# Four graph layers on one core: products copied by ScalarE, parts summed by TensorE, roots by Newton steps on VectorE, and one more tick between steps

## The chip, the cores and the metric

The kernel runs on one core of a Trainium2 chip. The metric is the device time of one launch in microseconds (us), taken as the median of several runs. PE is TensorE, PEld its weight loads, DVE VectorE, ACT ScalarE, POOL GpSimd and SP SyncE.

## The reference

Four graph networks run one after the other on 50,000 nodes of 256 numbers, each as `x = layernorm(x + net(x))`; all share one list of 25,000 edges. The first is a hypergraph net, the second and the fourth are two graph attention (GAT) convolutions each, the third is a graph convolution with batch norm. One GAT convolution:

```python
h = (x @ W).reshape(n, HEADS, HID)
e = leaky_relu(a_s[src] + a_d[dst], 0.2)
m = segment_max(e, dst); ex = exp(e - m[dst])
alpha = ex / segment_sum(ex, dst)[dst]
out = segment_sum(h[src] * alpha[:, :, None], dst) + b
```

The second net puts `elu` behind both of its convolutions. In the fourth the first convolution ends in a layernorm and a relu, and the second has one head.

## The kernel before

Nodes are kept in 98 tiles of 512 rows (128 partitions x J = 4 rows x 256 numbers, fp32). Region 0 (49 tiles) holds the nodes that edges point to, in the order of the edges; region 1 (49 tiles) the nodes that no edge points to, so they need no neighbours. `ORDER` mixes the two regions, mostly by turns. Edges are worked in 25 batches of up to 8 columns, two tiles of region 0 each.

After two hypergraph phases and two phases of node work, the program has five calls of `layer_phase`, each a `Block` of its own in which all engines start together: **l1** (kind `l1a`: second net, softmax sum and elu of its first convolution, and the product with the weights of its second), **l2** (`l1b`: sum and elu of the second, residual, layernorm), **l3** (`gcn`), **l5** (`l3a`: fourth net, sum, layernorm, relu, product) and **l6** (`l3b`: last sum, residual, layernorm, rows scattered to the output). Between l3 and l5 runs a phase of node work alone.

In a layer phase each engine runs its own program over a common count of ticks. The table `L` of class `Nodes` gives each stage of a tile its tick: tile u is at stage s in tick u + L[s]. No engine waits at a tick's end; it waits only on semaphores of other engines' steps. If a result is asked for in the same tick in which it is made, the asking engine usually waits; one tick later it usually does not. On DVE the steps of a tick are generators, and `take_turns` issues one instruction of each by turns, so that a step in a chain of dependent ones lies beside others.

Stages of a tile: `load` (SP); `pre` (ACT scales half of the tile's own rows by their share, L2283, DVE the other half, L2356, and DVE weighs the neighbours' sum into `part`, L2352, and adds it, L2371); ACT's exp for elu (L2261); `body` (elu L2395, in l2 also the residual L2405; row statistics L2421); `var` and `norm` (the variance, its root as `pow` on POOL L2135, DVE's `shifts` L2443, then ACT's normalized rows `z` L2248); `turn` and `zt` (PE transposes, ACT copies them, L2231); `prod` (PE, L2170, two halves of PSUM, `pm`); `evict` (out of PSUM: DVE with a bias row `row_b` in l1, L2454 and L2456; ACT in l5); `store` (SP, in l6 POOL's scatters, L2142).

Edges, batch b at tick `at(b)`: POOL gathers rows (L1667, each a software DMA for 128 rows), DVE makes the logits and running maxima at `at - 3` (L1824 to L1844), ACT their exps (L1733), DVE weighs and accumulates (L1865, L1881), ACT copies the maxima beside the sums at `at + 1` (L1737), SP stores them at `at + 2`, DVE makes the shares.

## Time and profile before

| | |
|---|---|
| median of 3 runs | 7084.83 us (7073.76 to 7100.17) |
| the profiled execution, its own time | 7096.27 us |
| its span, first to last instruction | 7094.5 us |
| DVE busy | 4901.1 us, 69% of the span |
| POOL busy | 3995.6 us, 56% |
| PE busy | 3822.3 us, 54% |
| ACT busy | 3205.9 us, 45% |
| mean granted PE clock | 0.799 |

Busy shares over the whole span hide that the phases have different limits; they are read phase by phase below. In the windows each row is a stretch of the span with each engine's busy us and its count of instructions, the granted PE clock (0.50 is 1.2 GHz, 1.00 is 2.4 GHz), the mean share of the DMA engines, and GB/s. One fp32 matmul of the program shows as two MATMUL rows, a transpose as one.

### The profile page before, as it was taken

To read this page: it belongs to the slowest core of one execution; us is meant where nothing else is said; L and a number is where in the kernel's file an instruction comes from. 1 tells how busy PE (TensorE), PEld (TensorE's weight loads), DVE (VectorE), ACT (ScalarE), POOL (GpSimd) and SP (SyncE) were. 2 spreads that over 40 slices of the span, in tenths; PEclk is the share of its full clock that TensorE was granted. 3 is DMA by queue.
4 is the path that set the end of the run, shared out by engine and by line. 5 is a ranking of instruction groups with operands and counts; after the bars stand their busy time and mean duration, and the time that the engine had idled before them with its cause. 6 is when DMAs were issued, how large, how long until landed. Compare 5 with 4: busy or idle time off the path is not lost. (4 is left out here: it accounts for less than half of the span.)

```text
span 7094.5 us, 77303 instructions
## 1 busy us (share of the span) xinstructions
PE 3822.3 (54%) x18205; PEld 3003.3 (42%) x18205; DVE 4901.1 (69%) x15616; ACT 3205.9 (45%) x7082; POOL 3995.6 (56%) x3216
## 2 busy tenths in 40 slices
PE   3568881068885887477700005998885677600000
PEld 1257770057774666366600002546774566500000
DVE  6635454634456776799799996866665999576664
ACT  0023330023333554355445555768885788633333
POOL 4767776757774887544065525621112555278887
PEclk9789995589997998799955557999998899855555
DMA  8744446945446997777578878989996677576665
GB/s 306 283 93 77 76 69 206 382 86 78 75 69 209 350 349 284 210 257 263 185 261 291 290 260 287 382 296 330 332 336 221 232 250 240 178 254 224 231 223 191
DMA packets 646102, 1633.93 MB, mean 230 GB/s; under 512 B 128454, under 2 KB 283878, under 8 KB 630290
## 3 DMA queue, kind: packets, MB, share of 16 engines
q1 hardware_dynamic: 459954, 1234.83, 49.9%
q0 software_dynamic: 185696, 394.18, 20.7%
q8 instruction: 150, 2.46, 0.2%
q14 instruction: 302, 2.47, 0.1%
HBM read 816.50 MB, written 813.62 MB: 230 GB/s over the span
## 5 line engine op out<-in xcount | busy, mean ns | idle before, releaser
L1708 PE MATMUL l_pb<-l_jx,k_ones 128*128 128x128 f32 x26 | 7.0, 446 | 1520.8 <-DVE l_jx L1941 1520.8
L802 POOL DMA_INDIRECT NS<-e_tot,e_idx x392 | 648.4, 1654 | 292.2 <-ACT e_tot L1060 221.2
L2248 ACT ACTIVATE l_z<-l_a,l_nb,l_rs 128x256 f32<-128x256 f32 x1176 | 609.8, 598 | 394.3 <-DMA out_dram<-l_z,k_ids 382.0
L1667 POOL DMA_INDIRECT l_eg<-HBT,k_nsrc x392 | 497.8, 1270 | 366.4 <-POOLq L142 129.8
L1708 PEld LDWEIGHTS l_pb<-l_jx,k_ones 128*128 128x128 f32 x26 | 5.8, 326 | 1521.5 <-DVE l_jx L1941 1521.5
L936 DVE TENSOR_SCALAR e_eq<-e_pk,z_skey 128x128 f32<-128x128 f32 x588 | 203.8, 347 | 632.2 <-DMA NS<-e_tot,e_idx 606.6
L2135 POOL TENSOR_TENSOR l_rs<-l_ve,k_minus_half 128x8 f32<-128x8 f32 x147 | 279.5, 1901 | 447.6 <-ACT l_z L2248 327.1
L2142 POOL DMA_INDIRECT out_dram<-l_z,k_ids x392 | 420.5, 1073 | 119.4 <-issue 109.7
L2170 PE MATMUL l_pm<-k_w_L3b,l_zt 128*128 128x258 f32 x1568 | 404.4, 416 | 130.3 <-ACT l_o L2218 115.2
L1203 POOL DMA_INDIRECT XH<-n_o,z_home x392 | 401.3, 1024 | 120.2 <-issue 113.5
L1060 ACT ACTIVATE e_tot<-e_pa 128x520 f32<-128x520 f32 x196 | 118.5, 604 | 755.5 <-DMA NS<-e_tot,e_idx 743.2
L2421 DVE BATCH_NORM_STATS2 l_bs<-l_a 128x6 f32<-128x256 f32 x1176 | 447.1, 406 | 1.7
L2170 PE MATMUL l_pm<-k_w_L1b,l_zt 128*128 128x264 f32 x1568 | 403.6, 406 | 79.6 <-DVE l_o L2456 76.7
L2283 ACT ACTIVATE l_a<-l_a,l_eshare 128x64 f32<-128x64 f32 (+1 forms) x1372 | 379.6, 365 | 100.1 <-DVE l_eshare L1923 72.5
L1881 DVE SCALAR_TENSOR_TENSOR l_erun<-l_erun,k_same,l_eg 128x260 f32<-128x260 f32 (+2 forms) x880 | 417.8, 475 | 4.0
L1227 PE MATMUL n_pm<-z_w_L1a,n_zt 128*128 128x264 f32 x1568 | 397.9, 410 | 15.1 <-DVE n_o L1265 9.5
L1667 POOL DMA_INDIRECT l_eg<-XH,k_psrc x196 | 236.6, 1207 | 299.8 <-DVEq L1886 239.7
L2170 PEld LDWEIGHTS l_pm<-k_w_L3b,l_zt 128*128 128x128 f32 x1568 | 321.0, 210 | 191.7 <-issue 141.1
L1011 PE MATMUL e_po<-z_w_e2n,e_hid 128*128 128x256 f32 x1584 | 381.1, 384 | 24.5 <-DVEq L899 24.5
L1420 POOL TENSOR_TENSOR n_rs<-n_ve,k_minus_half 128x8 f32<-128x8 f32 x49 | 80.2, 1637 | 538.2 <-DVE n_ve L1539 538.2
L1020 PE MATMUL e_pr<-e_zt,z_w_n2e 128*128 128x256 f32 x1584 | 376.2, 380 | 0.7 <-issue 0.3
L2170 PEld LDWEIGHTS l_pm<-k_w_L1b,l_zt 128*128 128x128 f32 x1568 | 297.6, 198 | 160.8 <-DVE l_o L2456 74.8
(384 smaller groups left out, 13058.2 us busy)
## 6 DMA issues: line engine op xcount, KB each, us to landing
NS<-z_zero SPq DMA_DIRECT2D x200, 520.0 KB
HBT<-l_o SPq DMA_DIRECT2D x196, 528.0 KB
l_a<-HBT SPq DMA_DIRECT2D x196, 528.0 KB, 7.2
GSUMS<-l_erun SPq DMA_DIRECT2D x72, 1056.0 KB
l_a<-XH SPq DMA_DIRECT2D x98, 528.0 KB
HA<-n_o SPq DMA_DIRECT2D x98, 528.0 KB, 7.9
l_a<-HA SPq DMA_DIRECT2D x98, 528.0 KB, 4.3
n_r<-NS SPq DMA_DIRECT2D x98, 520.0 KB
```

The costliest lines, as they stand in the source:

```text
L802: pool.indirect_dma_start(out=nodes, out_offset=bass.IndirectOffsetOnAxis(ap=idx[q % DEEP][:, k:k + 1], axis=0), in_=tot[q % 2][:, k, :], ...
L1011: mm = pe.matmul(po[:, k, :], hid[q % 2][:, i, k * P:(k + 1) * P], w2[:, i, 0:D], start=i == 0, stop=i == KC - 1)
L1020: mm = pe.matmul(pr[:, n, :], w1[:, i, n * P:(n + 1) * P], zt[q % 2][:, i].rearrange("p j n -> p (j n)"), start=i == 0, stop=i == KC - 1)
L1203: pool.indirect_dma_start(out=T["XH"], out_offset=bass.IndirectOffsetOnAxis(ap=S["home32"][:, col:col + 1], axis=0), in_=o[t % RO][:, j, : ...
L1227: last = pe.matmul(pm[h][:, i, 0:RW], zt[t % 2][:, k, h * (J // 2) + i, :], weight[:, k, :], start=k == 0, stop=k == KC - 1)
L1667: pool.indirect_dma_start(out=self.g[b % self.ng][:, k, :], out_offset=None, in_=self.table, in_offset=bass.IndirectOffsetOnAxis(ap=self.i ...
L1881: lk.link(dve.scalar_tensor_tensor(rt[:, k, 0:n], before, S["same"][:, b * BC + k:b * BC + k + 1], g[:, k, 0:n], ALU.mult, ALU.add))
L2142: pool.indirect_dma_start(out=self.out, out_offset=bass.IndirectOffsetOnAxis(ap=S["ids32"][:, col:col + 1], axis=0), in_=self.z[u % self.r ...
L2170: last = pe.matmul(self.pm[h][:, i, 0:self.wc], zt[:, k, h * (J // 2) + i, :], self.weight[:, k, 0:self.wc], start=k == 0, stop=k == KC - 1)
L2248: last = act.activation(z[:, j, 0:D], a[:, j, 0:D], ACT.Identity, bias=self.nb[b][:, col:col + 1], scale=self.rs[b][:, col:col + 1])
L2283: last = act.activation(a[:, j, f], a[:, j, f], ACT.Copy, scale=sh[:, 0, t % 2 * J + j, h:h + 1])
L2421: self.stat_lk.link(dve.bn_stats(bs[:, u % 2 * J + j, :], a[:, j, 0:D]))
```

## The change

- **l1**: the products leave PSUM by ACT copies (`evict` now for every kind but none on DVE). The bias row `row_b` is no longer added to them. Since shares sum to 1, the bias is added later: to the target's logits at the start of l2 (`logit_b`, one DVE add over `asd`), and to the rows in l2's sum.
- **l2**: PE adds own rows, `part` and `row_b` into PSUM tiles `ps` (two buffers) by matmuls with the identity and with a row of ones. ACT's exp and DVE's elu read `ps`. PE's sum of tile u waits for the elu of tile u - 2.
- **l6**: the `pow` on POOL becomes `root` on DVE: a first guess from the bits and four Newton steps, 13 instructions for each pair of tiles. l2 and l5 keep `pow` on POOL.
- **Ticks**: `sum` is a stage of its own, one tick after the weighing (`weigh`), in l1, l2 and l6; l5 had that already. With it exp, elu and all behind them come a tick later in l1, l2 and l6. On the edges ACT's exps move from `at - 3` to `at - 2`, the copy of the maxima from `at + 1` to `at + 2`, SP's store of the sums from `at + 2` to `at + 3`, and the own exponents on DVE a tick earlier.

The diff, cut to its core:

```diff
+                dve.tensor_tensor(S["logit_b"][:, HEADS:2 * HEADS], S["row_b"][:, D:D + HEADS], S["row_b"][:, D + HEADS:RW], ALU.add)
...
+    def copy_at(self, b):
+        return self.at(b) + 2 if b < NBAT - 1 else self.at(b) + 1
...
-            if tick == self.at(b) + 2:
+            if tick == (self.copy_at(b) + 1 if self.heads else self.at(b) + 2):
                 if self.heads:
                     sp.wait_ge(self.s_mc, b + 1)
...
-            if tick == self.at(b) - 3:
+            if tick == self.at(b) - 2:
                 g, x = self.g[b % self.ng], self.view(self.x[b % 2], w)
                 act.wait_ge(self.s_x, b + 1)
...
-            if self.heads and tick == self.share_at(b):
+            if self.heads and tick == (self.share_at(b) - 1 if b < NBAT - 1 else self.share_at(b)):
                 parts.append(self.own_exponents(dve, b))
...
+        if self.bias is not None:
+            lk.link(dve.tensor_tensor(S["asd"][:], S["asd"][:], over_columns(self.bias[:], C), ALU.add))
+            lk.settle(dve)
+            dve.sem_inc(self.s_ad, 1)
...
-        body = L["body"] = pre + 3 if self.elu else pre
-        self.split = kind == "l3a"
-        if self.split:
-            body = L["body"] = L["join"] = pre + 1
+        L["sum"] = pre + 1 if self.gat else pre
+        if self.elu:
+            L["exp"] = pre + 2
+        body = L["body"] = pre + 4 if self.elu else L["sum"]
...
-        if self.norm:
+        if self.norm and self.kind != "l3b":
             q = self.pair(tick, "var", 1)
...
+        now = self.tile(tick, "sum") if self.summed else None
+        if now:
+            u, region, t = now
+            ps, a = self.ps[u % 2], self.a[u % self.ra]
+            if u >= 2:
+                pe.wait_ge(self.s_elu, u - 1)
+            pe.wait_ge(self.s_in[u % self.ra], self.loaded(u))
+            if region == 0:
+                pe.wait_ge(self.s_sum, t + 1)
+                pe.wait_ge(self.s_self, t + 1)
+            for h in range(2):
+                js = slice(h * (J // 2), (h + 1) * (J // 2))
+                pe.matmul(ps[:, js, :], S["ident"][:], a[:, js, 0:D], start=True, stop=False)
+                if region == 0:
+                    pe.matmul(ps[:, js, :], S["ident"][:], self.part[t % 2][:, js, :], start=False, stop=False)
+                last = pe.matmul(ps[:, js, :], S["ones"][0:1, :], over_columns(S["row_b"][0:1, 0:D], J // 2), start=False, stop=True)
+            last.then_inc(self.s_ps, 1)
...
-        now = self.tile(tick, "evict") if self.mat and kind != "l1a" else None
+        now = self.tile(tick, "evict") if self.mat else None
...
+    def root(self, dve, q):
...
+        lk.link(dve.tensor_scalar(y[:].bitcast(I32), v[:].bitcast(I32), -0.5, float(0x5F3759DF), ALU.mult, ALU.add))
+        yield
+        for n in range(4):
+            lk.settle(dve)
+            lk.link(dve.tensor_tensor(w[:], y[:], y[:], ALU.mult))
+            yield
+            lk.settle(dve)
+            lk.link(dve.scalar_tensor_tensor(w[:], w[:], -0.5, v[:], ALU.mult, ALU.mult))
+            yield
+            lk.settle(dve)
+            ins = dve.scalar_tensor_tensor(y[:], w[:], 1.5, y[:], ALU.add, ALU.mult)
...
-        for h in range(2):
-            dve.wait_ge(self.s_m, 2 * u + h + 1)
-            js = slice(h * (J // 2), (h + 1) * (J // 2))
-            if region == 0:
-                dve.tensor_tensor(S["asd"][:, J * t + h * (J // 2):J * t + (h + 1) * (J // 2), :], self.pm[h][:, :, D:RW],
-                                  over_columns(S["row_b"][:, D:RW], J // 2), ALU.add)
-            dve.tensor_tensor(o[:, js, :], self.pm[h][:, :, 0:RW], over_columns(S["row_b"][:], J // 2), ALU.add).then_inc(self.s_o, 1)
-            yield
```

What ACT issues in two ticks in the middle of l1, before (`pt` and `zt` are the transposed tile, `ee` the exp):

```order
L2231 ACTIVATE l1_zt0<-l1_pt0 128x512
L2231 ACTIVATE l1_zt0<-l1_pt1 128x512
L2261 ACTIVATE l1_ee0<-l1_a2,k_minus_one 128x1024
L2283 ACTIVATE l1_a4<-l1_a4,l1_eshare1 128x64 x8
L2231 ACTIVATE l1_zt1<-l1_pt0 128x512
L2231 ACTIVATE l1_zt1<-l1_pt1 128x512
L2261 ACTIVATE l1_ee1<-l1_a3,k_minus_one 128x1024
```

and after (`pm` is the product in PSUM, `o` the rows to store, `asd` the logits):

```order
L2256 ACTIVATE l1_o2<-l1_pm0 128x528
L2256 ACTIVATE l1_o2<-l1_pm1 128x528
L2269 ACTIVATE l1_zt1<-l1_pt0 128x512
L2269 ACTIVATE l1_zt1<-l1_pt1 128x512
L2302 ACTIVATE l1_ee1<-l1_a5,k_minus_one 128x1024
L2324 ACTIVATE l1_a8<-l1_a8,l1_eshare1 128x64 x8
L2254 ACTIVATE k_asd<-l1_pm0 128x16
L2256 ACTIVATE l1_o0<-l1_pm0 128x528
L2254 ACTIVATE k_asd<-l1_pm1 128x16
L2256 ACTIVATE l1_o0<-l1_pm1 128x528
L2269 ACTIVATE l1_zt0<-l1_pt0 128x512
L2269 ACTIVATE l1_zt0<-l1_pt1 128x512
```

Copies out of PSUM now stand ahead of each tile's transposed rows: two for a product of region 1, four for one of region 0. In l2 before, PE has only the work at the phase's start and at the last batch (`pc`, `pb`):

```order
L1698 MATMUL l2_pc<-k_asd,k_spread_in 128x4
L1708 MATMUL l2_pb<-l2_jx,k_ones 128x128 x4
L1713 MATMUL l2_pb<-k_ident,l2_jx 128x128 x4
L1718 MATMUL l2_pc<-l2_hp,l2_jxt 128x64
L1719 MATMUL l2_pc<-l2_hp,l2_jxt 128x1
```

In l2 after, it sums each tile, here one of region 0 and one of region 1 (`part` are the weighed neighbours):

```order
L2182 MATMUL l2_ps0<-l2_a8,k_ident 128x512
L2184 MATMUL l2_ps0<-l2_part0,k_ident 128x512
L2185 MATMUL l2_ps0<-k_row_b,k_ones 128x512
L2182 MATMUL l2_ps0<-l2_a8,k_ident 128x512
L2184 MATMUL l2_ps0<-l2_part0,k_ident 128x512
L2185 MATMUL l2_ps0<-k_row_b,k_ones 128x512
L2182 MATMUL l2_ps1<-l2_a9,k_ident 128x512
L2185 MATMUL l2_ps1<-k_row_b,k_ones 128x512
L2182 MATMUL l2_ps1<-l2_a9,k_ident 128x512
L2185 MATMUL l2_ps1<-k_row_b,k_ones 128x512
```

So a tile of region 0 has six matmuls of 512 columns, one of region 1 four. POOL in the middle of l6, before (`rs` is the root):

```order
L2142 DMA out_0_dram<-l6_z0,k_ids32 50000x256 x4
L1667 DMA l6_eg0<-HBT,k_nsrc32 128x264 x2
L2135 TENSOR_TENSOR l6_rs0<-l6_ve0,k_minus_half 128x8
L2142 DMA out_0_dram<-l6_z1,k_ids32 50000x256 x4
L1667 DMA l6_eg0<-HBT,k_nsrc32 128x264 x2
```

and after:

```order
L2163 DMA out_0_dram<-l6_z2,k_ids32 50000x256 x4
L1674 DMA l6_eg0<-HBT,k_nsrc32 128x264 x2
L2163 DMA out_0_dram<-l6_z0,k_ids32 50000x256 x4
L1674 DMA l6_eg0<-HBT,k_nsrc32 128x264 x2
L2163 DMA out_0_dram<-l6_z1,k_ids32 50000x256 x4
```

Only DMA issues are left on POOL there.

## Rows read from the trace of the kernel before

**Rows 1.** Windows of the five changed or neighbouring phases, with its columns

```profile
core 0: us, PE busy (x) PEld busy (x) DVE busy (x) ACT busy (x) POOL busy (x), PEclk, DMA share, GB/s
2845.00:3533.00 688.00, 493.16 (x2382) 393.76 (x2382) 600.81 (x1254) 319.03 (x788) 237.56 (x197) 0.91 0.70 233
3533.00:4302.00 769.00, 7.33 (x30) 6.49 (x30) 740.40 (x2041) 423.74 (x1082) 370.44 (x246) 0.50 0.78 272
...
5444.00:6162.00 718.00, 490.34 (x2382) 417.65 (x2382) 646.41 (x1994) 540.84 (x1376) 345.29 (x246) 0.86 0.65 222
6162.00:7094.00 932.00, 3.26 (x9) 2.35 (x9) 570.24 (x2022) 297.86 (x690) 734.65 (x638) 0.50 0.65 224
```

**Rows 2.** Windows within the l1 phase: filling, running, after the last edges

```profile
2845.00:2900.00 55.00, 0.59 (x2) 0.50 (x2) 29.90 (x66) 4.25 (x15) 36.48 (x31) 0.50 0.78 152
3150.00:3200.00 50.00, 39.90 (x192) 30.94 (x190) 47.34 (x102) 25.82 (x69) 19.59 (x17) 0.97 0.73 256
3450.00:3500.00 50.00, 47.21 (x248) 41.08 (x249) 31.94 (x72) 20.59 (x38) 0.00 (x0) 0.93 0.53 166
```

**Rows 3.** Groups of instructions in the l1 phase: busy, mean ns, idle before

```profile
L2456 DVE TENSOR_TENSOR l_o<-l_pm,k_row_b 128x528 f32<-128x528 f32 x196 | 137.1, 699 | 35.6 <-PE l_pm L2170 35.5
```

**Rows 4.** The waits of the l1 phase: total us, times, longest

```profile
ACT l_eg L1733 <- DVE l_ex L1844: 123.9, 25, 62.5
PE l_pm L2170 <- DVE l_o L2456: 76.7, 81, 1.6
```

**Rows 5.** Timeline of the l1 phase: start, us, engine, line

```profile
3208.79 1.07 ACT L2231 ACTIVATE l_zt<-l_pt 128x512 f32<-128x512 f32 x2
3209.74 1.15 ACT L2261 ACTIVATE l_ee<-l_a,k_minus_one 128x1024 f32<-128x1024 f32 x1
3210.78 2.01 ACT L2283 ACTIVATE l_a<-l_a,l_eshare 128x64 f32<-128x64 f32 x8
```

**Rows 6.** Groups over the whole run: ACT copies out of PSUM

```profile
L1468 ACT ACTIVATE n_o<-n_pm 128x528 f32<-128x528 f32 x196 | 118.6, 605 | 58.1 <-PE n_pm L1451 58.1
L1467 ACT ACTIVATE k_asd<-n_pm 128x16 f32<-128x16 f32 x98 | 17.4, 178 | 45.6 <-PE n_pm L1451 45.6
```

**Rows 7.** A window of the l2 phase while it runs evenly

```profile
3700.00:3800.00 100.00, 0.00 (x0) 0.00 (x0) 99.87 (x279) 54.86 (x142) 55.84 (x36) 0.50 0.83 297
```

**Rows 8.** Groups of instructions in the l2 phase

```profile
L2371 DVE TENSOR_TENSOR l_a<-l_a,l_part 128x1024 f32<-128x1024 f32 x49 | 59.1, 1205 | 2.1 <-ACT l_a L2283 1.8
```

**Rows 9.** Groups over the whole run: DVE from PSUM, PE 512 wide

```profile
L1522 DVE TENSOR_TENSOR n_a<-n_a,n_py 128x1024 f32<-128x1024 f32 x98 | 117.8, 1202 | 4.9 <-PE n_py L1432 4.9
L2161 PE MATMUL l_pm<-l_zt,k_w_L 128*128 128x512 f32 x784 | 355.0, 596 | 0.0
```

**Rows 10.** A window of the l3 phase, 512-wide products

```profile
4500.00:4600.00 100.00, 100.00 (x372) 54.37 (x371) 84.20 (x160) 71.52 (x143) 64.36 (x52) 1.00 1.02 378
```

**Rows 11.** Groups of instructions in the l6 phase

```profile
L2142 POOL DMA_INDIRECT out_dram<-l_z,k_ids x392 | 420.5, 1073 | 119.4 <-issue 109.7 <-ACT l_z L2248 6.9 <-DVE l_nb L2443 2.2
L1667 POOL DMA_INDIRECT l_eg<-HBT,k_nsrc x196 | 225.4, 1150 | 95.3 <-issue 59.3 <-POOLq L142 36.1
L2135 POOL TENSOR_TENSOR l_rs<-l_ve,k_minus_half 128x8 f32<-128x8 f32 x49 | 87.7, 1789 | 1.9 <-DVE l_ve L2436 0.9
```

**Rows 12.** Timeline of POOL in the l6 phase

```profile
6510.41 1.02 POOL L1667 DMA_INDIRECT l_eg<-HBT,k_nsrc  x1 [0.30 <-issue]
6511.44 1.68 POOL L2135 TENSOR_TENSOR l_rs<-l_ve,k_minus_half 128x8 f32<-128x8 f32 x1
6513.31 1.95 POOL L2142 DMA_INDIRECT out_dram<-l_z,k_ids  x1 [0.19 <-issue]
```

**Rows 13.** Timeline of DVE at the start of l2: small steps, each needing the last

```profile
3552.18 0.19 DVE L1829 SCALAR_TENSOR_TENSOR l_ex<-l_ex 128x32 f32<-128x32 f32 x1
3552.41 0.19 DVE L1832 TENSOR_TENSOR l_exm<-l_ex,l_ead 128x32 f32<-128x32 f32 x1
```

**Rows 14.** A window of the l5 phase while it runs evenly

```profile
5600.00:5700.00 100.00, 75.47 (x362) 63.71 (x360) 99.58 (x312) 84.09 (x220) 59.55 (x44) 0.90 0.76 255
```

More of the change, by code:

```diff
@@ L1571, with __init__ @@
 class Edges:
-    def __init__(self, nc, S, s, table, tw, index, acc, heads, first, load=None):
+    def __init__(self, nc, S, s, table, tw, index, acc, heads, first, load=None, bias=None):
+        self.bias, self.s_ad = bias, s.sem("target_logits_biased")
         self.S, self.table, self.tw, self.index, self.heads, self.load, self.acc = S, table, tw, index, heads, load, acc
@@ L1785, in target_logits @@
         own, cap = self.own, self.cap
+        if self.bias is not None:
+            lk.link(dve.tensor_tensor(S["asd"][:], S["asd"][:], over_columns(self.bias[:], C), ALU.add))
+            lk.settle(dve)
+            dve.sem_inc(self.s_ad, 1)
         lk.link(dve.tensor_tensor(own[:], S["asd"][:, :, 0:H], S["asd"][:, :, H:2 * H], ALU.add))
@@ L2034, in __init__ @@
             self.s_dd = s.sem("squares_ready")
+        self.summed = kind == "l1b"
+        if self.summed:
+            self.ps = [s.ps(f"ps{b}", [P, J, D]) for b in range(2)]
+            self.s_ps = s.sem("rows_summed")
+            self.s_elu = s.sem("elu_ready")
         if self.elu:
@@ L2043, in __init__ @@
             self.nb = [s.sb(f"nb{b}", [P, 2 * J]) for b in range(2)]
+            self.rt = [s.sb(f"rt{b}", [P, 2 * J]) for b in range(2)]
+            self.root_lk = Links(s.sem("root_steps"))
             self.stat_lk = Links(s.sem("row_stats_ready"))
@@ L2071, in __init__ @@
                 self.wc = RW if kind == "l1a" else D + 2
+    place = SPOT
     def ticks(self):
@@ L2251, in scalar @@
         if self.elu:
-            u = tick - self.L["pre"] - 1
+            u = tick - self.L["exp"]
             if 0 <= u < len(ORDER):
                 (region, t), a = ORDER[u], self.a[u % self.ra]
-                if region == 0:
+                if self.summed:
+                    act.wait_ge(self.s_ps, u + 1)
+                elif region == 0:
                     act.wait_ge(self.s_sum, t + 1)
@@ L2259, in scalar @@
                 if u >= 2:
-                    act.wait_ge(self.s_u, u - 1)
-                act.activation(self.ee[u % 2][:], a[:, :, 0:D], ACT.Exp, bias=S["minus_one"][:]).then_inc(self.s_ee, 1)
+                    act.wait_ge(self.s_elu if self.summed else self.s_u, u - 1)
+                v = self.ps[u % 2][:] if self.summed else a[:, :, 0:D]
+                act.activation(self.ee[u % 2][:], v, ACT.Exp, bias=S["minus_one"][:]).then_inc(self.s_ee, 1)
         u = tick - self.L["pre"] + 1
@@ L2298, in vector @@
             return parts
-        now = self.tile(tick, "evict") if self.kind == "l1a" else None
-        if now:
-            parts.append(self.evict(dve, *now))
         if self.norm:
@@ L2305, in vector @@
                 parts.append(self.shifts(dve, q))
+            q = self.pair(tick, "var", 2) if self.kind == "l3b" else None
+            if q is not None:
+                parts.append(self.root(dve, q))
             q = self.pair(tick, "var")
@@ L2311, in vector @@
             parts.append(self.body(dve, *now))
-        now = self.tile(tick, "join") if self.split else None
-        if now and now[1] == 0:
-            parts.append(self.join_parts(dve, *now))
+        now = self.tile(tick, "sum")
+        if now and now[1] == 0 and not self.summed:
+            parts.append(self.sum_up(dve, *now))
         now = self.tile(tick, "pre")
-        if now and now[1] == 0:
-            parts.append(self.sum_up(dve, *now))
+        if now and now[1] == 0 and self.heads > 1:
+            parts.append(self.weigh(dve, *now))
         return parts
@@ L2330, in prepare, with weigh @@
         dve.drain()
[L2332 removed]
+    def weigh(self, dve, u, region, t):
         H, lk, e = self.heads, self.sum_lk, self.edges
         hw, b, k0 = D // H, t // 2, t % 2 * J
[L2335 removed]
+        sh, a, sa, part = e.share[b % 2], self.a[u % self.ra], self.self_act, self.part[t % 2]
         run = e.run[b % e.nrun][:, k0:k0 + J, 0:D]
@@ L2338, in sum_up @@
         dve.wait_ge(e.s_nw, b + 1)
-        dve.wait_ge(self.s_in[u % self.ra], self.loaded(u))
-        sa = self.self_act
-        if H == 1:
-            dve.wait_ge(self.s_self, t + 1)
+        if t >= 2:
+            if self.summed:
+                dve.wait_ge(self.s_ps, SPOT[t - 2] + 1)
+            else:
+                dve.wait_ge(self.s_sum, t - 1)
+        if sa < J:
+            dve.wait_ge(self.s_in[u % self.ra], self.loaded(u))
+            own = by_head(a[:, sa:J, 0:D])
+            lk.link(dve.tensor_tensor(own, own, spread(sh[:, 0, k0 + sa:k0 + J, :], hw), ALU.mult))
+            yield
+        ins = dve.tensor_tensor(by_head(part[:]), by_head(run), spread(sh[:, 1, k0:k0 + J, :], hw), ALU.mult)
+        if self.summed:
+            ins.then_inc(self.s_sum, 1)
+        else:
+            lk.link(ins)
+        yield
+    def sum_up(self, dve, u, region, t):
+        lk, e, a = self.sum_lk, self.edges, self.a[u % self.ra]
+        b, k0 = t // 2, t % 2 * J
+        dve.wait_ge(self.s_self, t + 1)
+        if self.heads == 1:
+            run, sh = e.run[b % e.nrun][:, k0:k0 + J, 0:D], e.share[b % 2]
             for j in range(J):
@@ L2348, in sum_up @@
         else:
-            part = self.part[t % 2]
-            if t >= 2:
-                dve.wait_ge(self.s_sum, t - 1)
-            lk.link(dve.tensor_tensor(by_head(part[:]), by_head(run), spread(sh[:, 1, k0:k0 + J, :], hw), ALU.mult))
-            yield
-            if sa < J:
-                own = by_head(a[:, sa:J, 0:D])
-                lk.link(dve.tensor_tensor(own, own, spread(sh[:, 0, k0 + sa:k0 + J, :], hw), ALU.mult))
-                yield
-            if self.split:
-                return
-            yield from self.add_parts(dve, u, t)
+            lk.settle(dve)
+            dve.tensor_tensor(a[:, :, 0:D], a[:, :, 0:D], self.part[t % 2][:], ALU.add).then_inc(self.s_sum, 1)
         if self.elu:
@@ L2394, in body @@
             dve.wait_ge(self.s_ee, u + 1)
-            elu = dve.scalar_tensor_tensor(a[:, :, 0:D], self.ee[u % 2][:], 1.0, a[:, :, 0:D], ALU.min, ALU.max)
+            v = self.ps[u % 2][:] if self.summed else a[:, :, 0:D]
+            elu = dve.scalar_tensor_tensor(a[:, :, 0:D], self.ee[u % 2][:], 1.0, v, ALU.min, ALU.max)
             if self.kind == "l1a":
@@ L2398, in body @@
                 return
-            lk.link(elu)
+            elu.then_inc(self.s_elu, 1)
             yield
-            lk.settle(dve)
+            dve.wait_ge(self.s_elu, u + 1)
             r = self.r[u % self.rr]
```

53 lines of the change are left out of this document (24 added, 29 removed).

## Prediction

> **What bounds the kernel now.** I read windows first, since a share over the whole span mixes phases with different limits: one row for each phase of attention layers [rows 1]. l1 takes 688 us with DVE busy 600.81 and PE 493.16; l2 takes 769 with DVE 740.40; l5 718 with DVE 646.41 and ACT 540.84; l6 932 with POOL 734.65 and DVE only 570.24. l3 and all before l1 are not touched (three small DVE steps in the setup, under 1 us), so the change is worth what these four rows lose.
>
> Then windows inside l1 [rows 2]. PE starts after about 55 us. In an even stretch DVE is busy 47.34 of 50 us and PE does 192 matmul rows, 24 to a tile (16 of the product, 8 transposes), so 8 tiles: 6.25 us a tile, set by DVE. Once the edges are through, PE does 248 rows in 50 us, 4.84 us a tile, with 47.21 us busy: that is PE's own pace.
>
> **l1: products copied by ACT.** DVE loses 196 copies of 699 ns, 137.1 us [rows 3], and 98 small ones, so it comes to about 450 of work and is no limit any more. PE waited 76.7 us for these copies, and ACT 123.9 us for logits asked for in the tick that makes them [rows 4]; the tick on the edges removes that. ACT's own pace then counts. A tick of region 0 has own rows 2.01, two transposed halves 1.07, exp 1.15 [rows 5], and now two copies of 605 ns and two of 178 [rows 6]; with 0.23 for the edges this makes 6.03 us. A tick of region 1 lacks own rows and small copies: 3.66. The mean, 4.85, equals PE's 4.84. But PE and ACT are tied within a tick: PE's product waits for ACT's copy of the half of `pm` before it, and ACT's transposed halves wait for PE. So I take the slower of the two in each: 49 x 6.03 + 49 x 4.84 = 533 us. With 55 ahead, 5 for the extra tick and 7 at the end: 600 us, **-88**. Bounds: PE alone, 98 x 4.84 = 474 + 67 = 541, **-147**; and, if each tile loses another 0.7 us to hand-overs, near 668, **-20**. DMA doesn't forbid it: share 0.73 at 6.25 us a tile is 4.6 us a tile.
>
> **l2: parts summed by PE.** In an even stretch DVE is busy 99.87 of 100 us [rows 7], so each us taken from it is taken from the phase. It loses 49 adds of 1205 ns, 59.1 us [rows 8]; as queued instructions overlap by some 0.07 us, 55 is what they hold. The elu now reads PSUM. A DVE instruction of this size with a PSUM operand takes 1202 ns [rows 9], so that costs nothing. The Trainium skill (VectorE: DVE Perf Modes, the section on the TRN2 errata) speaks against it: it gives a VectorE instruction that reads PSUM 62 cycles more than one that reads SBUF; by that 98 elus would cost about 6 us (an estimate from that page), and l2 would gain 6 us less. The trace does not agree: 1202 ns against 1205. Added are the bias add at the start (1,568 columns, about 2.5 us, nothing hides it) and one tick of filling, say 4. Sum: -55 + 7 = **-48**.
>
> What hides the 980 matmul rows (49 x 12 + 49 x 8) is PE's idleness, if it is fast enough. At 512 columns one row costs 355.0 us / 784 = 0.453 us at the high clock [rows 9], there with PE never idle [rows 10]. So 5.4 us for region 0 and 3.6 for region 1, 444 us in a phase of some 720: PE busy 62%. In l1 and l5 PE was busy 72% and 68% and its granted clock was 0.91 and 0.86 [rows 1], so I expect the high level most of the time. The two `ps` buffers give the loop elu(u-2), sum(u), exp(u), elu(u) two ticks, about 14.6 us, for 5.4 + 1.15 + 1.2. ACT gets half a tick late by waiting for the sum, but what it makes for the edges is wanted a tick later. If the cover goes, see the second rival.
>
> **l6: roots on DVE.** Here POOL is the limit. 392 scatters and 196 gathers hold 420.5 + 119.4 and 225.4 + 95.3 us with the gaps between them, and 49 roots 87.7 [rows 11]: together more than the 932 us of the phase, as spans on POOL overlap a little. In the timeline the root takes the place of a gap of 0.30 us: gather until 6511.43, root, next scatter at 6513.31 [rows 12]. So a root costs POOL 1.79 + 0.2 - 0.3 = 1.7 us, 84 for 49. DVE gains 637 steps of eight columns. In a dependent chain that stands alone a small step starts every 0.23 us [rows 13], 147 us; between others in the queue less than half. 570 + 147 is 717 of 850, so DVE hides even the dear case. The scatters may stretch: POOL's issues took 1073 and 1150 ns in the mean [rows 11] against 1.02 alone and 1.95 beside a busy DVE [rows 12]. That stretch is some 50 us in all; a DVE busier by a quarter adds 10, at most 35. The tick adds 3. Sum: -84 + 13 = **-71** (bounds -84 and -45). The Trainium skill (GPSIMD Engine Reference, section 1, Specifications) says that GpSimd contends with DVE instructions of two SBUF inputs, and 12 of the 13 Newton steps are such; it gives no price, so it changes neither number.
>
> **l5** keeps its work. In an even stretch DVE is busy 99.58 of 100 us [rows 14], so ACT's freedom from waits on the edges shortens only the end: **-5** (0 to -20). The moved steps on the edges are otherwise worth nothing where DVE or POOL is the limit. SP's store of the sums stands a tick later ahead of the loads, still some eight ticks before its buffer is wanted.
>
> **Sum.** 7096 - 88 - 48 - 71 - 5 = **6884 us**, against the profiled execution's 7096.27. The median of the runs is 11 us lower (0.2%), less than their spread, so I leave it there.
>
> **Rivals.**
> - *PE and ACT find their full pace in l1* (-147), and l5's end shortens by 20: 7096 - 147 - 48 - 71 - 20 = 6810. For it: queues smooth a tick of 6.03 against one of 3.66. Against it: `pm` has one buffer for each half. 16 in 100.
> - *PE stays at the low clock in l2.* It has gaps of 1.8 to 3.7 us in each tick, and before this the phase was at 0.50 throughout [rows 1]. At half the rate its rows cost 888 us; with 63 for filling 951, +182, and with a hand-over of 0.4 us for each tile 990, +221: 7096 + 221 - 88 - 71 - 5 = 7153, slower. It decides from l2 above 968 us, 9.3 us of PE a tile. Against it: at the low level PE would never be idle, and in l1 such stretches had the clock at 0.91. 3 in 100 for this; 3 more for the half of it that ends near 7110. The Trainium skill (TensorE: Matmul & The Clock Gate, Part 1) says that the clock is released by activity and falls back in idleness; l2's 0.50 with an idle PE agrees.
> - *ACT comes too late.* It now waits in l1 for PE and in l2 for the sum, and a tick less of slack lies between the edges' exps and DVE. l1 gains 45 rather than 88, l2 20, l6 45: 7096 - 110 - 5 = 6980. For it: ACT was busy 84.09 of 100 us in l5 and PE waited for it there [rows 14]. 20 in 100.
> - *The change does nothing in l6*, because DMA writes, not POOL's issues, pace the scatters: 6955. Against it: DMA share 0.65 [rows 1]; l3 reached 1.02 [rows 10]. 5 in 100, within the range.
>
> **How the numbers follow.** My forecast has 53 in 100, with 6840 to 6930 as its own range. The first, third and fourth rival are still faster; with them the range is 6795 to 6985, leaving out 2 in 10. About 0.5% (35 us) is what a measurement of this kernel can tell from no change. Faster by more: 0.93; same: 0.04; slower: 0.03.
>
> **What would show it.** l1's window near 600 us with DVE below 80% and PE above 80%; l2's near 720 with DVE above 95% busy, about 980 more rows on PE and a clock well above 0.50; l6's near 860 with POOL still without a pause and DVE at 75 to 85%; l5 within 20 of 718. I am wrong if DVE waits in l2 for ACT's exp or edge weights, if PE in l2 is at 0.50, or if POOL's scatters take much over 1.1 us.

## The result, and the profile after

| | kernel before | changed kernel |
|---|---|---|
| median of the runs of the comparison, us | 7083.74 | 7005.9 |
| range of the runs, us | 7073.76 to 7100.17 (4) | 6992.02 to 7028.68 (4) |
| span of the profiled execution, us | 7094.5 | 7026.9 |

The ratio is 0.9888, 95% interval [0.9871, 0.9904]: faster by 78 us, where I forecast 212. The time lies above my range, which ended at 6985.

I cut both traces where each phase clears its running sums (the DVE memset of `l_erun`), and the last phase at the span's end. A phase is the distance from one such row to the next, so it includes the hand-over. The windows in [rows 1] were cut by eye and differ from this by up to 9 us. The last column is the changed kernel run again in a later comparison, and is used further down.

| phase | before | changed | difference | forecast | changed, run again |
|---|---|---|---|---|---|
| ahead of l1 | 2848.1 | 2854.2 | +6.2 | 0 | 2764.8 |
| l1 | 688.9 | 560.9 | -128.0 | -88 | 561.9 |
| l2 | 773.7 | 849.4 | +75.7 | -48 | 851.4 |
| l3 and what lies behind it | 1136.1 | 1133.8 | -2.3 | 0 | 1122.3 |
| l5 | 718.8 | 708.7 | -10.1 | -5 | 708.9 |
| l6 | 929.0 | 919.9 | -9.1 | -71 | 855.2 |
| sum | 7094.5 | 7026.9 | -67.6 | -212 | 6864.5 |

First the windows of the five phases of the changed kernel, l1 to l6, which answer to [rows 1] (the third is l3):

```profile
core 0: us, PE busy (x) PEld busy (x) DVE busy (x) ACT busy (x) POOL busy (x), PEclk, DMA share, GB/s
2853.00:3415.00 562.00, 458.27 (x2382) 389.84 (x2382) 470.90 (x964) 419.92 (x1082) 298.87 (x197) 0.92 0.87 285
3415.00:4264.00 849.00, 749.80 (x1010) 217.91 (x1010) 690.18 (x1990) 419.01 (x1082) 332.07 (x246) 0.65 0.75 248
4264.00:5398.00 1134.00, 982.00 (x4708) 697.30 (x4708) 746.03 (x1733) 833.51 (x1568) 321.91 (x247) 0.97 0.92 321
5398.00:6107.00 709.00, 490.92 (x2383) 416.87 (x2383) 645.15 (x1991) 541.29 (x1376) 355.49 (x246) 0.87 0.65 225
6107.00:7026.00 919.00, 2.73 (x8) 1.86 (x7) 650.15 (x2658) 293.67 (x690) 650.75 (x589) 0.50 0.65 227
```

In l2 DVE lost 50 us of work (740 to 690), as planned, and the phase is longer all the same. PE, which was idle there, is now busy 749.80 of 849 us, at a mean granted clock of 0.65, that is, for most of the time at the lower of its two levels (1.2 GHz of 2.4). In l6 POOL lost 84 us of work and the phase 9.

Next, windows of 100 us: one in l1 and one in l2 while they run evenly, which answer to the second of [rows 2] and to [rows 7], and then four that follow one another in l6:

```profile
3100.00:3200.00 100.00, 94.14 (x485) 79.77 (x486) 98.81 (x202) 89.48 (x241) 70.05 (x45) 0.98 0.99 340
3700.00:3800.00 100.00, 91.25 (x130) 26.54 (x128) 88.09 (x260) 56.23 (x146) 39.27 (x30) 0.70 0.84 270
6200.00:6300.00 100.00, 0.00 (x0) 0.00 (x0) 77.80 (x320) 37.33 (x88) 78.64 (x71) 0.50 0.74 257
6300.00:6400.00 100.00, 0.00 (x0) 0.00 (x0) 70.71 (x287) 30.11 (x72) 67.72 (x62) 0.50 0.62 215
6400.00:6500.00 100.00, 0.00 (x0) 0.00 (x0) 62.29 (x239) 29.61 (x68) 68.72 (x63) 0.50 0.63 213
6500.00:6600.00 100.00, 0.00 (x0) 0.00 (x0) 83.82 (x353) 37.33 (x88) 78.64 (x71) 0.50 0.74 254
```

l1 does 485 matmul rows in 100 us, 24 to a tile: 4.95 us a tile, where it was 6.25. The four rows of l6 are the first sign of what happened there. In two of them POOL does 71 instructions and DVE 320 or 353; in the two between, 62 or 63 and 287 or 239. One phase, the same loop, two paces.

Now the groups of instructions of l2, sums first (busy, mean ns, idle before):

```profile
L2182 PE MATMUL l_ps<-l_a,k_ident 128*128 128x512 f32 x392 | 332.5, 944 | 71.5 <-DVE l_a L2431 47.2 <-DVE l_part L2391 23.9
L2185 PE MATMUL l_ps<-k_row_b,k_ones 1*128 1x512 f32 x392 | 301.3, 857 | 0.0
L2184 PE MATMUL l_ps<-l_part,k_ident 128*128 128x512 f32 x196 | 154.0, 883 | 0.0
...
L2431 DVE SCALAR_TENSOR_TENSOR l_a<-l_ee,l_ps 128x1024 f32<-128x1024 f32 x98 | 117.5, 1199 | 29.7 <-ACT l_ee L2302 29.6
L2302 ACT ACTIVATE l_ee<-l_ps,k_minus_one 128x1024 f32<-128x1024 f32 x98 | 109.1, 1113 | 375.5 <-PE l_ps L2185 360.6 <-issue 14.8
```

There are 980 rows, as counted beforehand, but their times add up to 787.8 us (they overlap a little: PE is busy 749.80 us in the whole phase) and not to 444. ACT's exp waits 360.6 us for them in 93 of the 98 tiles. The elu out of PSUM takes 1199 ns, so that part of the forecast held.

The PE timeline of l2 (start, us, engine, line) shows when the clock moves. What counts is the shape behind the names: L2185 multiplies from one partition (1x512), the others from 128.

```profile
3702.90 1.20 PE L2185 MATMUL l_ps<-k_row_b,k_ones 1*128 1x512 f32 x2
3704.03 1.12 PE L2182 MATMUL l_ps<-l_a,k_ident 128*128 128x512 f32 x2
3705.08 1.12 PE L2185 MATMUL l_ps<-k_row_b,k_ones 1*128 1x512 f32 x2
3706.14 1.75 PE L2182 MATMUL l_ps<-l_a,k_ident 128*128 128x512 f32 x2
3707.81 2.07 PE L2185 MATMUL l_ps<-k_row_b,k_ones 1*128 1x512 f32 x2
3712.23 2.08 PE L2182 MATMUL l_ps<-l_a,k_ident 128*128 128x512 f32 x2 [2.35 <-DVE l_a L2431]
```

From 3702.90 PE runs at the high level, a pair of rows in 1.05 us. At 3706.14 it falls back to the low one, 1.75 and then 2.07 us for a pair. It had not paused: in this trace the rows follow one another without a gap from 3677.11 on. The one pause in these rows, 2.35 us, comes after the fall. So idleness did not lower the clock here, and I had taken idleness for the only thing that could.

Last, l6. Its POOL groups answer to the first two of [rows 11], and the third row is one of DVE's three Newton steps:

```profile
L2163 POOL DMA_INDIRECT out_dram<-l_z,k_ids x392 | 423.9, 1081 | 166.4 <-issue 117.2 <-ACT l_z L2286 48.9 <-DVEq L1899 0.3
L1674 POOL DMA_INDIRECT l_eg<-HBT,k_nsrc x196 | 225.8, 1152 | 123.9 <-issue 58.9 <-POOLq L142 36.2 <-DVEq L1899 28.8
...
L2492 DVE SCALAR_TENSOR_TENSOR l_rs<-l_rt,l_rs 128x8 f32<-128x8 f32 x196 | 31.1, 159 | 34.1 <-remote 16.8 <-DVE l_rt L2489 9.0 <-issue 5.4
```

POOL's issues did not stretch (1081 and 1152 ns, before 1073 and 1150), and the roots are gone from it. New are its waits: 48.9 us for ACT's `l_z` (6.9 before) and 28.8 for DVE's queue. DVE's timeline in one of the slow windows shows where these begin:

```profile
6432.10 0.16 DVE L1842 SCALAR_TENSOR_TENSOR l_ex<-l_ex 128x8 f32<-128x8 f32 x1
6433.44 0.17 DVE L2486 TENSOR_TENSOR l_rt<-l_rs 128x8 f32<-128x8 f32 x1 [1.18 <-remote]
6433.53 0.17 DVE L2466 BATCH_NORM_AGGREGATE l_mv<-l_bs 128x2 f32<-128x6 f32 x1
6434.15 0.18 DVE L2466 BATCH_NORM_AGGREGATE l_mv<-l_bs 128x2 f32<-128x6 f32 x1 [0.44 <-issue]
6434.85 0.48 DVE L2405 SCALAR_TENSOR_TENSOR l_a<-l_erun,l_eshare,l_a 128x256 f32<-128x256 f32 x1 [0.53 <-issue]
```

DVE pauses by about half a microsecond before instructions that wait for nothing: the second `BATCH_NORM_AGGREGATE` needs only statistics that were ready long before. What releases it is "issue" or a queue that the profile can't name. Between 6400 and 6480 there are 47 gaps of over 0.12 us, 37 us in sum; between 6500 and 6580 there are 4, of 4.3 us. POOL in the first 80 us keeps its regular 0.30 between issues. The delay reaches it behind them, through ACT:

```profile
6479.30 0.16 DVE L2504 SCALAR_TENSOR_TENSOR l_nb<-l_mv,l_rs 128x8 f32<-128x8 f32 x1
6479.49 2.07 ACT L2286 ACTIVATE l_z<-l_a,l_nb,l_rs 128x256 f32<-128x256 f32 x4 [3.88 <-DVE l_nb L2504]
6482.40 1.02 POOL L2163 DMA_INDIRECT out_dram<-l_z,k_ids  x1 [11.73 <-ACT l_z L2286]
```

POOL stands idle for 11.73 us until ACT has made `l_z`, and ACT could not start it before DVE's late `l_nb`.

Pauses of this kind are not DVE's alone. I count the gaps over 0.12 us that the profile puts down to "issue" or to a queue that it can't name. In l6 of this trace DVE has 98 of them (115 us) and ACT 24 (129 us), where the changed kernel run again has 22 (35 us) and none. Ahead of l1, where the kernels do not differ, the kernel before has 138 on DVE, 54 on ACT and 66 on PE in its trace of the first comparison, the changed kernel 160, 53 and 96; each of the 13 later traces has 15 or 16 on DVE and none on ACT and PE. So what disturbs l6 disturbed both kernels and three engines in the first comparison.

### The profile page after: what moved, and what is told of

The parts are those of the page before. It is cut to its first block and busy times, and to the rows that moved or that the text cites. A ratio compares the mean times of both kernels' runs of the same rounds, so it can differ in the third digit from the quotient of the medians.

```text
span 7026.9 us, 79868 instructions
## 1 busy us (share of the span) xinstructions
PE 4531.4 (64%) x19185; PEld 3208.0 (46%) x19185; DVE 4798.5 (68%) x15913; ACT 3296.5 (47%) x7376; POOL 3935.7 (56%) x3167
## 5 line engine op out<-in xcount | busy, mean ns | idle before, releaser
L1674 POOL DMA_INDIRECT l_eg<-HBT,k_nsrc x392 | 462.4, 1180 | 386.3 <-DVEq L1899 146.6
L2163 POOL DMA_INDIRECT out_dram<-l_z,k_ids x392 | 423.9, 1081 | 166.4 <-issue 117.2
L2156 POOL TENSOR_TENSOR l_rs<-l_ve,k_minus_half 128x8 f32<-128x8 f32 x98 | 187.4, 1912 | 470.8 <-ACT l_z L2286 267.1
L2208 PEld LDWEIGHTS l_pm<-k_w_L3b,l_zt 128*128 128x128 f32 x1568 | 320.8, 210 | 191.8 <-issue 140.6
L2208 PE MATMUL l_pm<-k_w_L1b,l_zt 128*128 128x264 f32 x1568 | 375.0, 393 | 28.8 <-ACT l_o L2256 28.2
L2182 PE MATMUL l_ps<-l_a,k_ident 128*128 128x512 f32 x392 | 332.5, 944 | 71.5 <-DVE l_a L2431 47.2
L1674 POOL DMA_INDIRECT l_eg<-HA,k_nsrc x196 | 260.7, 1330 | 198.1 <-DVEq L1899 96.7
```

The lines of the kernel that those rows point to most:

```text
L1674: pool.indirect_dma_start(out=self.g[b % self.ng][:, k, :], out_offset=None, in_=self.table, in_offset=bass.IndirectOffsetOnAxis(ap=self.i ...
L2163: pool.indirect_dma_start(out=self.out, out_offset=bass.IndirectOffsetOnAxis(ap=S["ids32"][:, col:col + 1], axis=0), in_=self.z[u % self.r ...
L2208: last = pe.matmul(self.pm[h][:, i, 0:self.wc], zt[:, k, h * (J // 2) + i, :], self.weight[:, k, 0:self.wc], start=k == 0, stop=k == KC - 1)
```

## The experiments

Thirteen runs followed, on four chips. Each is the changed kernel with the edit shown, if nothing else is said. Phases are cut as above. Ratios are to the kernel before on the same chip, where its median was between 6993.91 and 7002.69 us. The chip of the first comparison is not on record; that it was a fifth one is my inference from the times ahead of l1.

The code of l2 is the same in the changed kernel, its two repetitions, the first experiment and the one on l1; in these five traces l2 takes 836.3 to 851.4 us at a clock of 0.65 to 0.67. Smaller differences tell nothing.

### What holds l2: the bias product, a third tile, the identity

**The root back on GpSimd** (also the control for l1 and l2):

```
-        if self.norm and self.kind != "l3b":
+        if self.norm:
             q = self.pair(tick, "var", 1)
...
-            q = self.pair(tick, "var", 2) if self.kind == "l3b" else None
+            q = None
```

> The changed kernel with the root of the last layer (l6) back on GpSimd as pow; the new ticks stay. Theory A (l6 gained only 11 us, 932 to 921, because the Newton steps took from VectorE what GpSimd won): with the pow back, l6 is bound by GpSimd again and takes 925 to 940 us, and VectorE's idle times of 0.4 to 3 us between small steps are gone. Theory B (the extra tick or something else in l6 costs time and Newton's steps are fine): l6 takes 980 us or more, 60 to 80 above the 921 of the changed kernel. l2 stays near 849 us in both.

Measured: 6934.91 us, ratio 0.9905 [0.9888, 0.9922]; l1 561.0, l2 848.0, l5 707.1, l6 926.5. l6 is as in the kernel before. The profile of this run and that of the changed kernel then seemed to say that the root's move is worth 7 us.

**No bias product** (the bias is left out of the result):

```
-                last = pe.matmul(ps[:, js, :], S["ones"][0:1, :], over_columns(S["row_b"][0:1, 0:D], J // 2), start=False, stop=True)
```

> The changed kernel without the matmuls that add the bias row in l2, so the bias is left out of the result: 588 matmul rows on TensorE instead of 980. Theory A (l2 went from 769 to 849 us because TensorE's sums at a mean clock of 0.65 are its limit): l2 falls to 700 to 740 us, VectorE is busy over 95% of it again. Theory B (l2 is slow because of the chain elu, sum, exp, elu over two PSUM tiles, whatever the length of the sum): l2 stays above 800 us.

Measured: 6745.32 us, ratio 0.9637 [0.962, 0.9654]; l2 728.0. PE does 588 rows instead of 980. l2 is 46 us below the 774 of before. That is near my forecast, 48, but the forecast was made for all 980 rows.

**Three PSUM tiles for the sums in place of two:**

```
-            self.ps = [s.ps(f"ps{b}", [P, J, D]) for b in range(2)]
+            self.ps = [s.ps(f"ps{b}", [P, J, D]) for b in range(3)]
...
-            if u >= 2:
-                pe.wait_ge(self.s_elu, u - 1)
+            if u >= 3:
+                pe.wait_ge(self.s_elu, u - 2)
```

> The changed kernel with three PSUM tiles for l2's sums instead of two, so that a sum waits for the elu three tiles back. Theory A (TensorE is slow as its clock falls when it waits for the elu of two tiles back; with fewer such waits the clock stays high): mean clock of l2 above 0.8, l2 takes 710 to 770 us. Theory B (the clock does not follow the waits, TensorE is simply too slow for 980 rows): clock stays at 0.65 to 0.7 and l2 within 20 us of 849.

Measured: 6778.73 us, ratio 0.9682 [0.9666, 0.9698]; l2 756.6. The whole phase, and 100 us of it:

```profile
3336.00:4092.00 756.00, 673.27 (x1010) 198.34 (x1010) 687.65 (x1990) 420.72 (x1082) 341.25 (x246) 0.73 0.82 278
3700.00:3800.00 100.00, 96.35 (x140) 27.95 (x139) 99.93 (x290) 61.77 (x164) 53.29 (x38) 0.73 0.91 319
```

The phase is in the range of theory A, the clock in neither: 0.73, where A had over 0.8 and B at most 0.7. With the bias products from one partition left in, the third tile takes 91 us off l2 (848.0 to 756.6), and in an even stretch DVE is the limit again, 99.93 of 100 us, at this low clock.

**The bias through the identity, from 128 partitions.** The rows of `row_b` are equal on all partitions, so the identity gives the same sum as a row of ones from one partition:

```
-S["ones"][0:1, :], over_columns(S["row_b"][0:1, 0:D], J // 2), start=False, stop=True)
+S["ident"][:], over_columns(S["row_b"][:, 0:D], J // 2), start=False, stop=True)
```

> The changed kernel with the bias row of l2 added by a matmul of the identity with the bias row on all 128 partitions, instead of a row of ones with the bias row on one partition; as many matmul rows and columns. Theory C (the clock stays low because the one-partition matmuls, a third to a half of the rows, leave most of the array idle): mean clock of l2 rises above 0.8 and l2 falls below 780 us. Theory A (only waits matter): clock 0.65 to 0.7, l2 within 20 us of 849.

Measured: 6752.28 us, ratio 0.9643 [0.9626, 0.9659]; l2 737.7. The window of l2, with the same count of rows on PE:

```profile
3332.00:4070.00 738.00, 510.64 (x1010) 206.16 (x1010) 687.54 (x1991) 418.44 (x1082) 332.29 (x247) 0.88 0.85 285
```

The clock is 0.88 against 0.65, PE's busy time 510.64 us against 749.80, still more than the 444 of the forecast. No other instruction of the phase differs. PE also waits more for the elu here than in the changed kernel (172.2 us against 47.2), and its clock is the higher one nevertheless. The timeline (in the rows behind these, at the high level, the starts of pairs are 0.86 us apart):

```profile
3618.80 1.02 PE L2185 MATMUL l_ps<-k_row_b,k_ident 128*128 128x512 f32 x2
3623.34 2.07 PE L2182 MATMUL l_ps<-l_a,k_ident 128*128 128x512 f32 x2 [3.52 <-DVE l_a L2431]
3625.21 1.77 PE L2184 MATMUL l_ps<-l_part,k_ident 128*128 128x512 f32 x2
3626.81 1.02 PE L2185 MATMUL l_ps<-k_row_b,k_ident 128*128 128x512 f32 x2
```

After a pause of 3.52 us one pair and most of the next run low, and the third is high again.

**32 partitions, and one with the identity's first row.** Both keep the count and the columns of the products:

```
-S["ones"][0:1, :], over_columns(S["row_b"][0:1, 0:D], J // 2), start=False, stop=True)
+S["ident"][0:32, :], over_columns(S["row_b"][0:32, 0:D], J // 2), start=False, stop=True)
```

> The bias products go through the first 32 rows of the identity against the first 32 partitions of the bias row, so that the bias reaches the first 32 edges' rows of each tile only. The count and the columns of the products are the same. If the clock follows how many rows of the array are in use, it lies between 0.65 (one row) and 0.88 (128 rows), near 0.70, and l2 near 810 us. If it was the row of ones as the loaded operand (all of the output partitions written) that held the clock down, 0.88 and 738 us as with the whole identity.

> The bias products as in the changed kernel from one partition, but with the first row of the identity as the loaded operand in place of a row of ones, so that only one row of each tile gets the bias. If the clock follows the number of rows of the array in use, it is as with the row of ones: 0.65, l2 near 850 us. If the values that reach the outputs matter (128 outputs other than zero against one), the clock is lower still or higher, and l2 is off by over 10 us.

Measured, in one run each: with 32 partitions 6825.21 us, l2 819.2, clock 0.71; with one and the identity's first row 6860.66 us, l2 848.8, clock 0.66. The windows of l2, the first with 32 partitions, the second with one:

```profile
3323.00:4142.00 819.00, 700.19 (x1010) 205.70 (x1010) 688.67 (x1991) 418.32 (x1082) 331.57 (x247) 0.71 0.76 257
```

```profile
3330.00:4175.00 845.00, 744.22 (x1010) 216.65 (x1010) 686.42 (x1988) 419.03 (x1082) 328.47 (x245) 0.66 0.76 247
```

So with two tiles the clock of the phase follows how many partitions the bias products contract over, 1, 32 or 128: 0.66, 0.71, 0.88, for the same number of instructions and columns. The 819.2 us for 32 lie outside the 836.3 to 851.4 of l2 with one. What the loaded operand holds, a row of ones or a row of the identity, makes no difference that shows (848.8 us).

**Identity and three tiles together:** the two edits above in one kernel.

> Bias through the identity and three PSUM tiles for the sums together. The first alone brought l2 to 738 us, the second alone to 757, with the bias left out it was 728. If both cure the same thing (TensorE being late for the elu), the sum of the two is worth little more than the better one: l2 at 725 to 735, time 6735 to 6750 us. Rival: at the higher clock the third tile lets TensorE work without its pauses and DVE reaches the 720 of the forecast, 6730 us or less.

Measured: 6733.92 us, ratio 0.9614 [0.9597, 0.9631]; l2 720.9. This kernel beats both. A window of its l2:

```profile
3700.00:3800.00 100.00, 73.88 (x143) 30.38 (x143) 99.93 (x294) 62.46 (x166) 55.18 (x39) 0.88 0.90 309
```

And who waited for its sums (us, times), a wait of 360.6 us in the changed kernel and 257.4 with the identity alone:

```profile
who waited for it (us, times):
  ACT l_ee L2302: 19.0, 14
```

DVE is the limit again (99.93 of 100 us), as in [rows 7], with less to do in each tile. The two cures overlap: from the 848.0 of the control the identity alone takes 110 us, the third tile alone 91, both 127. Of the expectation the rival is right on l2, which reaches the 720 of my forecast; its time, 6730 or less, is missed by 4 us.

### What holds l6

**The changed kernel again,** in a later comparison, unchanged:

> The changed kernel as it is, beside the kernels of this call, on a chip on which the four experiments before had l6 at 852 to 856 us wherever DVE has the roots, while the changed kernel's own trace has 921. Theory A (something of that one chip or of that one set of runs held DVE up in l6): l6 near 855, ratio near 0.980 (6865 us beside 7003). Theory B (it belongs to this program, for example where its instructions lie): l6 near 920 again, ratio 0.989 to 0.990 (6925 to 6935). Both expect l2 near 849 and l1 near 561.

Measured: 6859.35 us, ratio 0.9793 [0.9775, 0.981]; phases in the table at the top: l6 855.2. Theory A. Two windows of l6 there; POOL is busy between 78.03 and 79.25 us in each of the six from 6109 to 6709. Below them POOL's two groups, idle for 225.4 us in sum, against 290.3 in the first trace and 214.7 in [rows 11]; the difference of the first two, 65 us, is the difference of the phases (919.9 and 855.2):

```profile
6209.00:6309.00 100.00, 0.00 (x0) 0.00 (x0) 78.70 (x325) 34.46 (x83) 78.33 (x72) 0.50 0.74 254
6309.00:6409.00 100.00, 0.00 (x0) 0.00 (x0) 74.93 (x306) 34.70 (x83) 78.64 (x71) 0.50 0.70 241
...
L2163 POOL DMA_INDIRECT out_dram<-l_z,k_ids x392 | 421.9, 1076 | 119.6 <-issue 115.4 <-ACT l_z L2286 4.3
L1674 POOL DMA_INDIRECT l_eg<-HBT,k_nsrc x196 | 228.8, 1167 | 105.8 <-issue 57.6 <-POOLq L142 36.1 <-DVEq L1899 10.8
```

And DVE at the same instructions of the program as in the timeline of l6 above:

```profile
6305.78 0.16 DVE L1842 SCALAR_TENSOR_TENSOR l_ex<-l_ex 128x8 f32<-128x8 f32 x1
6305.86 0.15 DVE L2486 TENSOR_TENSOR l_rt<-l_rs 128x8 f32<-128x8 f32 x1
6305.94 0.24 DVE L2466 BATCH_NORM_AGGREGATE l_mv<-l_bs 128x2 f32<-128x6 f32 x2
6306.09 0.45 DVE L2405 SCALAR_TENSOR_TENSOR l_a<-l_erun,l_eshare,l_a 128x256 f32<-128x256 f32 x1
```

From the start of L1842 to that of L2405 it takes 0.31 us here, and 2.75 us in the first trace, for the same four kinds of work.

**Identity, root on GpSimd:** the edits of the first and the fourth experiment together.

> The bias is multiplied through the identity on 128 partitions, and l6's roots are back on GpSimd. If the roots on DVE are what brings l6 to 852 (by freeing GpSimd of 49 roots), l6 is near 926 here, as in the run with the root alone back on GpSimd, and the time about 6752 + 74 = 6826 us. Rival: l6 is fast for another reason that came with the three other programs, and it stays near 855, 6755 us. l2 is near 738 in both.

Measured: 6814.26 us, ratio 0.9736 [0.9718, 0.9754]; l6 926.8, l2 735.1. With the fourth experiment (l6 852.4, on another chip) this gives the root's worth in l6: 74 us, where I had forecast 71. On one and the same chip the first experiment has 926.5 and the second to fourth 851.8 to 855.8, a difference of 71 to 75.

**Two Newton steps in place of four,** on the kernel with identity and three tiles:

```
-        for n in range(4):
+        for n in range(2):
```

> Three sum tiles, the bias through the identity, and two Newton steps instead of four in l6 (roots a little less exact). VectorE gets 294 instructions less. If GpSimd alone limits l6 where VectorE is not held up, l6 stays at 850 us and the time at 6734. Rival: VectorE's chain of small steps is part of l6's tick and it falls to 835 or less. On a chip where VectorE pauses before its instructions, as in the changed kernel's own trace, l6 would gain from the lower count: nearer 850 than 920.

Measured: 6727.38 us, ratio 0.962 [0.9604, 0.9636]; l6 853.0, against 849.9 with four. DVE did 2364 instructions in l6 instead of 2658, and the phase did not get shorter: DVE is not its limit there. The roots get less exact for nothing. Whether fewer steps help where the engines pause was not tried.

**The kernel before again, and the changed one a third time:**

> The kernel before, profiled beside the kernels of this call. Its trace stands so far from one chip alone, on which the phases ahead of l1 took 2848 us for this kernel and 2854 for the changed one, against 2757 to 2774 in all later traces. If that chip was slower for both, l1 starts near 2760 here, and its phases should be 689, 774, 1122, 719 and 927 us, in all near 6995. If l6 took longer on that chip for the kernel before too, l6 is below 920 here, and then the roots on VectorE gain less than the 72 us that I ascribe to them.

> The changed kernel a third time. If this chip is like the others of the experiments: phases of 561, 850, 1122, 709 and 855 us, 6860 in all, ratio 0.980. If it is like the one of the first comparison: VectorE pauses before its instructions in l6, l6 near 920, ratio 0.989, and the kernel before starts l1 near 2848 on it.

Measured: the kernel before 7003.91 us, with l1 starting at 2774.0 and phases of 686.1, 773.9, 1119.3, 719.2 and 929.9; the changed kernel 6842.08 us, ratio 0.9779 [0.975, 0.9807], with 561.7, 839.1, 1120.2, 708.9 and 853.8. The kernel before is not below 920 in l6: 929.9 here and 929.0 in the first comparison, so it lost nothing there. Both traces of it have about the same number of gaps over 0.12 us on DVE in 700 us of l6, 61 and 63; of those without a releaser ACT has 14 (68 us) in the first and none here. They cost POOL nothing.

### What made l1 faster than forecast

**The products copied by VectorE again,** as plain copies in `evict` (the bias stays with TensorE), all ticks as in the changed kernel:

```
-        now = self.tile(tick, "evict") if self.mat else None
+        now = self.tile(tick, "evict") if self.mat and kind != "l1a" else None
...
+            dve.tensor_copy(o[:, js, :], self.pm[h][:, :, 0:RW]).then_inc(self.s_o, 1)
```

> The changed kernel with l1's products copied by VectorE again (as plain copies, without the bias, which stays with TensorE in l2), and all the later ticks kept. If the gain of l1 (689 to 561 us) comes from taking the copies off VectorE, l1 is back near 680 and the time near 6859 + 120 = 6980 us. Rival: the later ticks on the edges, which remove ScalarE's waits for logits, made a part of it, and l1 lies between 600 and 650 us, 6900 to 6950. l2 and l6 stay at 850 and 855.

Measured: 6967.33 us, ratio 0.9964 [0.995, 0.9978]; l1 667.0, l2 836.3. l1 is back by 105 of its 127 us, so the move of the copies makes most of the gain and the later ticks some 20. The 667 us lie between the ranges of the two expectations. The copy takes 698 ns on DVE, as with the bias added (699).

## Why the prediction was wrong

The direction was right, and so were the mechanisms in l1, l5 and l6. The step that failed is in the part on l2: "What hides the 980 matmul rows [...] is PE's idleness, if it is fast enough. [...] so I expect the high level most of the time".

**l2, forecast -48, measured +76.** Three parts of the term held. DVE's work fell by 50 us; the elu out of PSUM takes 1199 ns; and once PE is in time, l2 is 720.9 us, 53 below before. What failed is the price of PE's rows: 444 us forecast, 787.8 measured. I took the clock from phases where every product contracts over 128 partitions (l1 and l5, [rows 1]) and laid it on a phase in which 392 of 980 rows contract over one. With nothing else changed, the same number of rows has a clock of 0.88 when the bias too comes from 128 partitions, and l2 falls from 849 to 738. The Trainium skill (TensorE: Matmul & The Clock Gate, Part 1), which I cited for a clock released by activity and lowered by idleness, fits the low rows behind the pause of 3.52 us; the fall at 3706.14, in a stretch without a pause, shows that being busy is not enough.

My second rival named the low clock, though not what causes it, at 3 to 6 in 100, and was half right. It had PE at the low level throughout and l2 at 990 us. But I argued against it that "at the low level PE would never be idle", as if that had to bring the clock back. It didn't: PE was busy 91.25 of 100 us at a clock of 0.70.

A second part was the two `ps` tiles. I reckoned that a loop of two ticks had room for 5.4 + 1.15 + 1.2 us. The third tile is worth 17 us with the identity (737.7 to 720.9) and 91 without it (848.0 to 756.6), where it also lifts the clock from 0.66 to 0.73. So the cover was thin at either clock, and the low clock alone does not explain l2: each of the two cures by itself brings it below the 774 of before. I had left out that PE begins a sum only when the elu of two tiles back is through: with two tiles ACT still waits 257.4 us for the sums, with three 19.0.

**l6, forecast -71, measured -9 here and -75 in the later comparisons.** The step was right: there three traces with the roots on POOL have l6 at 926.5 to 929.9 us, and nine with them on DVE at 849.9 to 855.8. POOL's issues stayed at 1.08 and 1.15 to 1.17 us. In the trace of the first comparison DVE and ACT pause before instructions that wait for nothing, in stretches of 100 to 200 us. POOL then waits for `l_z` and for DVE's queue, and the gain of the freed time is lost. The kernel before paused too in that comparison, but lost nothing in l6: 929.0 us there and 929.9 later. That it has 2022 DVE instructions in this phase against 2658 fits a DVE whose instructions come too slowly; whether the count decides was not shown, since the pauses did not come again. What pauses the engines stays open. The two instruction queues of the DMA moved as much in both traces of the changed kernel (158 and 307 packets), so more code fetched is not it. Both kernels also took 74 to 104 us more in the first comparison ahead of l1, where all three engines pause, and 12 to 17 in l3; the change does nothing in either.

**l1, forecast -88, measured -128.** Mis-sized. I took the slower of ACT and PE in each tick, 5.44 us in the mean; measured were 4.95 us a tile, near PE's own 4.84. The queues even out a long tick against a short one, as my first rival had it (-147, 16 in 100). The durations held: 612 and 185 ns for the copies on ACT, forecast 605 and 178.

**l5, forecast -5, measured -10.** Inside its bounds. **Ahead of l1 and l3:** no change, as said; 6 and 2 us are what two executions differ by.

**The sum.** With l2 as in the kernel with the identity and three tiles (-53), l1 at -128, l5 at -10 and l6 at -75, the change would have been worth 266 us. That kernel measured 6733.92 beside 7001.52, 268 less. In the first comparison the forecast's terms miss by +124 in l2 and +62 in l6, and by -40 in l1 and -5 in l5; the other phases add 4. That makes 144 (rounded), the distance between 212 and the traces' 67.6. In the later comparisons, with l6 undisturbed, the change was worth 142 and 152 us of its 212, less than my own range had it but inside the whole one (111 to 301 below). So l2 and the disturbed l6 carried the time out of the range together, and l1, faster than I had reckoned, hid 40 us of the miss.

## What to carry to other kernels

Work that is moved to an idle TensorE must be priced at the clock that this work itself gets, not at the one of another phase: here a phase with two products in five over one partition had a clock of 0.65, with the engine busy 9 parts in 10. To add a constant row on TensorE, spread it over all partitions and multiply by the identity; it has the same number of columns and here it saved 110 us of one phase. Where an engine is put in the loop between two others, give its output a tile more than the loop seems to need. And if one phase's gain is missing from a trace although each duration is as forecast, look at the same instructions in a second execution, on another chip, before explaining it.
